# Attention and routed feed-forward block: the first head group's rows made by tripled weights, batch 1 projected in step 0

## The chip, the cores and the metric

The kernel runs on one core of a Trainium2 chip. The metric is the device time of one execution in microseconds (us), given as the median of several executions. A core has five engines that work side by side, each through its own list of instructions in order: TensorE (PE in the profile; PEld is its loading of weights), VectorE (DVE), ScalarE (ACT), GpSimd (POOL) and SyncE (SP, which here only issues DMAs). They wait for each other through semaphores.

## The reference

A transformer block on x (4 batches, 256 tokens, 128 channels) with 64 context tokens per batch. All is float32.

```
q, k, v = heads(LN(x) @ W + b)                 # 16 heads of 8 channels
y  = softmax(causal(q k^T / sqrt(8))) v        # self attention
y += softmax(qc kc^T / sqrt(8)) vc             # keys and values from the context
x  = x + y @ Wp + bp
h  = LN(x); top 8 of 32 experts by sigmoid(h @ Wr + br)
x  = x + shared(h) + sum_e w_e * expert_e(h)   # silu(h Wg) * (h Wu) @ Wd
```

## The kernel before

Attention goes in 16 steps: step i is batch `b = i // 4` and head group `g = i % 4`, four heads at a time. For each step there are four products on TensorE: `natural(i)` gives scores with queries on the partitions, from which VectorE takes the row maxima (`maxima(i)`: three reductions, of self tile 0, self tile 1 and the context); `turn_max(i)` turns them, ScalarE's `shift(i)` writes them as four more rows of the queries; `scores(i, c)`, c = 0 to 3, gives the shifted scores with keys on the partitions, ScalarE takes the exponential (`exps`), POOL masks it; `attend_self` and `attend_context` multiply with the values. In the loop, step i of TensorE holds scores(i), turn_max(i+1), natural(i+2) and attend(i-1), and behind natural the work in `tail_at[i]`.

A number is kept as two halves of fewer bits, hi and lo. A product of two such is three products, hi*hi, hi*lo, lo*hi (`product3`). Queries and keys of a head group have only 32 channels, so the three products are stacked into one: `query_rows` and `key_rows` hold 96 rows, each channel three times with the halves that belong together, and 4 rows for the maxima. The rows are placed by DMA from `queries` and `keys`, three DMAs per group and kind, from the queues of SP, POOL and ScalarE. `expand(i)` then makes `key_blocks` for step i: a copy of the key rows for each of the four heads, with the other heads' rows multiplied by 0 of `head_mask`. VectorE (later POOL) does heads 0 and 1, ScalarE 2 and 3. `expand_ctx(g)` does the same for the context keys, once per group for all batches. The ring has four slots, so `expand(4)` is the block of step 4, the first of batch 1.

The queries, keys and values of batches 0 and 1 are projected ahead of the loop. ScalarE rounds to the hi half with the bias added (`round_qkc`), VectorE makes the lo half (`split_qkc`), and `place_batch` has SP place the rows. Batch 2 and 3 follow as tails: `x_pair` turns the four normed tiles of both, then `keys_queries` and `cross_values` project. `run_idle(n, bank)` is n matmuls of zeros, whose results nobody reads.

After the loop comes the routed feed-forward part, to which nothing is changed.

## Time and profile before

| what | us |
|---|---|
| median of 3 executions | 203.08 (202.93 to 204.57) |
| the profiled execution | 202.79 |
| its span (first to last instruction) | 201.0 |
| TensorE busy | 187.7 (93%) |
| VectorE busy | 151.2 (75%) |
| ScalarE busy | 137.0 (68%) |
| POOL busy | 111.5 (55%) |

The span is what the trace covers; the execution adds 1.79 us around it. All starts are counted from the span's beginning. Of the span the attention steps take the part up to about 105, the feed-forward part the rest.

### The profile page before, as it was taken

What the parts mean: (1) busy time and instruction counts of PE and PEld (TensorE: products, weight loads), DVE (VectorE), ACT (ScalarE), POOL (GpSimd) and SP (SyncE); (2) the same over time, 40 slices, a digit from 0 to 9 for tenths busy, and PEclk for the clock granted to TensorE, in tenths of its full rate; (3) what the DMA queues carried; (4) which work ended last, traced back from release to release, by engine and by line L of the source; (5) the groups of instructions that cost most, each with busy time, mean ns of one, the idle gap of its engine ahead of it and who ended that gap; (6) DMA issues with size and microseconds to landing.
All of it is one profiled execution on the core that took longest, in us unless ns stands there. A gap on an engine that the chain in (4) does not pass through costs nothing.

```text
span 201.0 us, 4004 instructions
## 1 busy us (share of the span) xinstructions
PE 187.7 (93%) x1254; PEld 138.2 (69%) x1254; DVE 151.2 (75%) x345; ACT 137.0 (68%) x276; POOL 111.5 (55%) x181
## 2 busy tenths in 40 slices
PE   7969999999999999989998999599799999999993
PEld 2537677777777677767674777388588888887662
DVE  2999997566578756995574699659867888887982
ACT  3546898787898879997779455665555656555571
POOL 7899994475595799659455476674512233000020
PEclk9999999999999999999999999999999999999998
DMA  4464323232352233301302112110000000000003
GB/s 112 107 154 122 104 73 85 55 76 77 75 127 66 71 81 93 92 0 42 78 5 49 29 39 55 44 41 2 2 0 3 0 0 0 0 2 3 0 0 104
DMA packets 20434, 10.40 MB, mean 52 GB/s; under 512 B 11881, under 2 KB 18542, under 8 KB 20414
## 3 DMA queue, kind: packets, MB, share of 16 engines
q1 hardware_dynamic: 19290, 9.24, 18.1%
q0 software_dynamic: 672, 0.69, 1.4%
q10 hardware_dynamic: 452, 0.23, 0.5%
q8 instruction: 10, 0.16, 0.4%
q14 instruction: 10, 0.08, 0.1%
HBM read 4.51 MB, written 0.52 MB: 25 GB/s over the span
## 4 chain that ended last, share of the span: by engine, by line
PE 67%; POOL 13%; issue 7%; DVE 6%; ACT 4%; DMA 1%; DVEq 0%; POOLq 0%; ACTq 0%
PE psum L1394 10%; PE psum L1395 9%; PE psum L1396 9%; PE psum L1495 5%; PE psum L1551 5%; PE psum L1588 4%; PE psum L1576 4%; POOL hid_lo L732 4%; PE psum L1598 3%; PE psum L1494 3%; PE psum L1556 3%; POOL ckey_rows L450 3%; PE psum L1724 2%; PE psum L1560 2%; POOL key_rows L436 2%
## 5 line engine op out<-in xcount | busy, mean ns | idle before, releaser
L968 ACT ACTIVATE gate<-psum,bias_cols 128x512 f32<-128x512 f32 (+2 forms) x35 | 23.6, 676 | 29.1 <-PE psum L1396 29.0
L836 ACT ACTIVATE probs<-psum 128x512 f32<-128x512 f32 x64 | 36.3, 596 | 2.3 <-PE psum L1556 1.2
L732 POOL TENSOR_TENSOR hid_lo<-hid,hid_hi 128x512 fp32r<-128x512 f32 x13 | 16.8, 1289 | 31.0 <-ACT hid_hi L977 30.9
L1338 DVE SCALAR_TENSOR_TENSOR gated<-psum,bias_cols,gate 128x512 f32<-128x512 f32 x32 | 24.0, 749 | 11.3 <-ACT gate L968 10.4
L1350 DVE TENSOR_TENSOR hid<-gated,psum 128x512 f32<-128x512 f32 x32 | 21.9, 683 | 3.1 <-PE psum L1724 1.1
L1495 PE MATMUL psum<-key_blocks,query_rows 96*128 96x512 f32 x48 | 24.1, 545 | 0.0
L651 POOL TENSOR_TENSOR w_late_lo<-w_ffn,w_late_hi 128x384 fp32r<-128x384 f32 x11 | 12.8, 1161 | 18.9 <-ACT w_late_hi L848 18.9
L977 ACT CAST hid_hi<-hid 128x512 fp32r<-128x512 f32 (+1 forms) x33 | 20.2, 613 | 3.5 <-PE psum L1396 1.8
L1131 DVE TENSOR_REDUCE row_max<-psum 128x4 fp32r<-128x512 f32 x16 | 11.0, 689 | 13.9 <-PE psum L1495 13.9
L1135 DVE TENSOR_REDUCE row_max<-psum 128x4 fp32r<-128x1024 f32 x16 | 19.4, 1215 | 0.0
L1394 PE MATMUL psum<-xT_hi,w_late_hi 128*128 128x512 f32 x42 | 16.8, 401 | 0.0
L1395 PE MATMUL psum<-xT_lo,w_late_hi 128*128 128x512 f32 x42 | 16.4, 391 | 0.0
L1396 PE MATMUL psum<-xT_hi,w_late_lo 128*128 128x512 f32 x42 | 16.4, 391 | 0.0
L687 POOL TENSOR_SCALAR_AFFINE_SELECT probs<-probs 128x512 f32<-128x512 f32 x16 | 10.2, 637 | 10.6 <-ACT probs L836 10.4
L843 ACT COPY o_sb<-psum 128x512 f32<-128x512 f32 x16 | 9.4, 586 | 9.3 <-PE psum L1588 9.2
L773 ACT ACTIVATE key_blocks<-key_rows,head_mask 100x256 fp32r<-100x256 f32 x32 | 14.4, 499 | 1.8 <-DMA key_rows<-keys 1.8
L1017 DVE TENSOR_TENSOR hid_lo<-hid,hid_hi 128x512 fp32r<-128x512 f32 (+2 forms) x22 | 14.4, 660 | 1.0 <-ACT hid_hi L977 0.9
L691 POOL TENSOR_SCALAR_AFFINE_SELECT probs<-probs 128x512 f32<-128x512 f32 x16 | 10.2, 636 | 8.4 <-ACT probs L836 8.2
L1494 PE MATMUL psum<-causal,ident_bf 128*128 128x512 bf16 x32 | 12.4, 389 | 1.8 <-DVE key_blocks L1037 1.6
L678 POOL TENSOR_TENSOR key_blocks<-key_rows,head_mask 100x256 fp32r<-100x256 f32 x22 | 13.2, 622 | 0.0
L1724 PE MATMUL psum<-routeT,spread 128*128 128x512 f32 x32 | 12.9, 404 | 0.0
L1551 PEld LDWEIGHTS psum<-query_rows,key_blocks 100*128 100x128 f32 x64 | 8.6, 188 | 5.2 <-issue 4.4
(205 smaller groups left out, 516.6 us busy)
## 6 DMA issues: line engine op xcount, KB each, us to landing
query_rows<-queries SPq DMA_DIRECT2D x46, 64.0 KB, 2.1
key_rows<-keys SPq DMA_DIRECT2D x39, 32.0 KB, 1.9
w_ffn<-in_L_ffn_Wg SPq DMA_DIRECT2D x16, 64.0 KB, 2.0
w_ffn<-in_L_ffn_Wu SPq DMA_DIRECT2D x16, 64.0 KB, 2.2
w_ffn<-in_L_ffn_Wd SPq DMA_DIRECT2D x16, 64.0 KB, 2.1
ckey_rows<-ckeys POOLq DMA_DIRECT2D x12, 32.0 KB, 2.1
key_rows<-keys POOLq DMA_DIRECT2D x9, 32.0 KB, 2.0
x_sb<-in_x SPq DMA_DIRECT2D x2, 128.0 KB, 2.5
```

What stands on the lines that cost most here:

```text
L732: pool.tensor_tensor(hid_lo[:, n % 3, :], hid[:, n % 3, :], hid_hi[:, n % 3, :].bitcast(F32), ALU.subtract).then_inc(pool_lo_done, 1)
L836: act.activation(probs[:, i % 2, c, :], bank(B_ST + c % 2), ACT.Exp, scale=SCALE).then_inc(exp_done, 1)
L968: act.activation(gate[rows_of(n), n % 3, part], psum[of, B_GATE + n % 2, part], ACT.Silu, bias=bias_cols[of, BIAS_GATE + u:BIAS_GATE + u + ...
L977: act.copy(hid_hi[rows_of(n - 1), (n - 1) % 3, :], hid[rows_of(n - 1), (n - 1) % 3, :]).then_inc(hid_rounded, 1)
L1135: dve.tensor_reduce(to[:, 1, :], psum[:, B_NAT1:B_NAT1 + 2, :].rearrange("p k (j c) -> p j k c", j=GROUP), AX.XY, ALU.max).then_inc(max_do ...
L1338: dve.scalar_tensor_tensor(out=gated[:, n % 3, :], in0=bank(B_UP + n % 2), scalar=bias_cols[:, BIAS_UP + u:BIAS_UP + u + 1], in1=gate[:, n ...
L1350: dve.tensor_tensor(hid[:, n % 3, :], gated[:, n % 3, :], bank(B_WIDE + n % 2), ALU.mult).then_inc(hid_done, 1)
L1394: pe.matmul(dst, w_hi, x_hi, start=start, stop=False, skip_group_check=True)
L1395: pe.matmul(dst, w_hi, x_lo, start=False, stop=False, skip_group_check=True)
L1396: return pe.matmul(dst, w_lo, x_hi, start=False, stop=stop, skip_group_check=True)
L1495: return pe.matmul(to, query_rows[0:KR, b % 2, g, 0, P * q:P * (q + 1)], blocks[:, :, P * k:P * (k + 1)], start=not diagonal, stop=True, s ...
L1551: ins = pe.matmul(psum[:, to, SEQ * j:SEQ * (j + 1)], key_blocks[0:ROWS, i % RING, 2 * c + j, 0:P], query_rows[0:ROWS, b % 2, g, 0, :], st ...
```

## The change

It touches the part ahead of the steps and the first three steps.

- For group 0 of batch 0 the rows are not placed by DMA. Weights for its 32 channels are written three times side by side (`w_direct_hi`, `w_direct_lo`, 96 columns per tensor), and `project_direct(k)` makes the 96 rows of keys, queries and cross queries by three products each. ScalarE's `round_direct` writes all rows as hi halves, VectorE's `split_direct` rewrites the 32 rows that want lo halves. The rows of a group now have another arrangement for g = 0, so `head_mask` has two versions; the biases are repeated (`first_bias`).
- Batch 1 is not projected ahead of the loop but as the tail of step 0; `x_pair` moves from step 0 to step 1, and batch 2 and 3 follow one step later than before.
- The maxima of step 0 are turned in two parts, self first (`first_turn`, `first_shift`), so scores(0, 0) wait for the first part only.
- Work is dealt out anew: the context copy, the bias copy and two norms go from VectorE to ScalarE, part of the weight split and heads 0 and 1 of `expand_ctx` from VectorE to POOL, the statistics of batches 2 and 3 go behind maxima(1). Placement of group 0's context keys and group 1 and 2's keys moves to SP, of group 1's queries to POOL. The masks are made before x has landed.

```diff
-        tail_at = {0: [("x_pair", FIRST_BATCHES)]}
-        for b in range(FIRST_BATCHES, BATCH):
-            tail_at[2 * b - 3] = [("keys_queries", b)]
-            tail_at[2 * b - 2] = [("cross_values", b)]
+        tail_at = {0: [("keys_queries", 1), ("cross_values", 1)], 1: [("x_pair", 2)]}
+        for b in range(2, BATCH):
+            tail_at[2 * b - 2] = [("keys_queries", b)]
+            tail_at[2 * b - 1] = [("cross_values", b)]
...
+            sp.wait_ge(ckey_rows_set, 1)
+            sp.wait_ge(ck_rounded, 1)
+            place_ctx_keys(sp, 0, (0, 1))
+            sp.wait_ge(ck_split, 1)
+            place_ctx_keys(sp, 0, (2,))
             sp.wait_ge(qkc_rounded, 1)
-            place_keys(sp, 0, 0, (0, 1))
+            place_keys(sp, 0, 1, (0, 1))
             sp.wait_ge(qkc_split, 1)
-            place_keys(sp, 0, 0, (2,))
+            place_keys(sp, 0, 1, (2,))
+            place_keys(sp, 0, 2)
             sp.wait_ge(qkc_split, 3)
-            place_queries(sp, 0, 0, (1,))
-            for g in range(1, GROUPS):
-                place_queries(sp, 0, g)
+            place_queries(sp, 0, 2)
+            place_ctx_keys(sp, 3)
+            place_keys(sp, 0, 3)
+            place_queries(sp, 0, 3)
             place_batch(sp, 1)
...
+            place_ctx_keys(pool, 1)
+            pool.wait_ge(qkc_rounded, 3)
+            place_queries(pool, 0, 1, (0, 2))
+            place_ctx_keys(pool, 2, (0,))
+            pool.wait_ge(qkc_split, 3)
+            place_queries(pool, 0, 1, (1,))
...
+            def round_direct(k):
+
+                to = (key_rows[0:SHIFT_ROW, 0, 0, :], query_rows[0:SHIFT_ROW, 0, 0, 0, :],
+                      query_rows[0:SHIFT_ROW, 0, 0, 1, :])[k]
+                bias = ORDER[k][1] + BIAS_DIRECT
+                act.wait_ge(m_direct, k + 1)
...
+            act.wait_ge(have_neg_mean, 1)
+            norm(2)
+            norm(3)
+            expand_ctx(0)
+            round_x(1)
+            first_shift(0)
+            expand(1)
+            exps(0, (0,))
+            first_shift(1)
+            exps(0, (1,))
             expand_ctx(1)
-            exps(0, (0, 1))
+            exps(0, (2, 3))
             expand(2)
...
+                if i == 1:
+                    act.wait_ge(have_neg_mean, 2)
+                    for t in range(4, TILES):
+                        norm(t)
...
+            def project_direct(k):
+
+                tensor = ORDER[k][0]
+                product3(psum[0:SHIFT_ROW, B_DIRECT[k], 0:SEQ], w_direct_hi[:, tensor, :], w_direct_lo[:, tensor, :],
+                         xT_hi[:, tokens(0)], xT_lo[:, tokens(0)]).then_inc(m_direct, 1)
...
             natural(0)
-            project(1)
-            turn_max(0)
-            run_idle(3, B_MISC)
+            run_idle(2, B_ST)
...
+            def first_turn(s):
+
+                pe.wait_ge(max_done, 2 + s)
+                if s:
+                    pe.wait_ge(shift_placed, 1)
+                for n in (2 * s, 2 * s + 1):
+                    ins = pe.matmul(psum[0:GROUP, B_MAX, P * n:P * (n + 1)], row_max[:, 0, n, :],
+                                    ident_r[:, :], start=True, stop=True)
+                ins.then_inc(t_max, 1)
```

On ScalarE, around the first exponentials (`probs`; `x` is a normed tile of x). Before:

```order
L780 ACTIVATE ckey_blocks<-ckey_rows,head_mask 100x4x64 [waits placed_ck1]
L780 ACTIVATE ckey_blocks<-ckey_rows,head_mask 100x4x64
L836 ACTIVATE probs<-psum 128x512 [waits m_st] x2
L773 ACTIVATE key_blocks<-key_rows,head_mask 100x256 [waits pool_placed_k2]
L773 ACTIVATE key_blocks<-key_rows,head_mask 100x256
L876 ACTIVATE x<-x_sb,neg_mean,rstd 128x128 [waits have_neg_mean]
L876 ACTIVATE x<-x_sb,neg_mean,rstd 128x128
L836 ACTIVATE probs<-psum 128x512 [waits m_st] x2
```

And now, from the two blocks of `expand(1)` on:

```order
L826 ACTIVATE key_blocks<-key_rows,head_mask 100x256 [waits placed_k0_1]
L826 ACTIVATE key_blocks<-key_rows,head_mask 100x256
L910 ACTIVATE probs<-psum 128x512 [waits m_st]
L902 CAST query_rows<-psum 4x256 [waits t_max]
L910 ACTIVATE probs<-psum 128x512 [waits m_st]
L835 ACTIVATE ckey_blocks<-ckey_rows,head_mask 100x4x64 [waits placed_ck1]
L835 ACTIVATE ckey_blocks<-ckey_rows,head_mask 100x4x64
L910 ACTIVATE probs<-psum 128x512 [waits m_st] x2
```

The context blocks of group 1 (`placed_ck1`), first of all before, now stand behind two exponentials and a shift, and these wait for TensorE (`m_st`, `t_max`).

On VectorE, behind the maxima of group 2, the first three rows of each. Before:

```order
L1131 TENSOR_REDUCE row_max<-psum 128x4 [waits m_nat,t_max]
L1140 TENSOR_REDUCE row_max<-psum 128x8 [waits m_nat]
L1135 TENSOR_REDUCE row_max<-psum 128x4 [waits m_nat]
L1017 TENSOR_TENSOR xT_lo<-psum,xT_hi 128x512 [waits xT_rounded]
L1037 TENSOR_SCALAR key_blocks<-key_rows,head_mask 100x256 [waits m_st,placed_k1_0]
L1037 TENSOR_SCALAR key_blocks<-key_rows,head_mask 100x256
```

And now:

```order
L1232 TENSOR_REDUCE row_max<-psum 128x4 [waits m_nat,t_max]
L1241 TENSOR_REDUCE row_max<-psum 128x8 [waits m_nat]
L1236 TENSOR_REDUCE row_max<-psum 128x4 [waits m_nat]
L1114 SCALAR_TENSOR_TENSOR neg_mean<-moments,rstd 128x4 [waits have_rstd]
L1176 SCALAR_TENSOR_TENSOR keys<-psum,bias_cols,keys 128x256 [waits qkc_rounded]
L1176 SCALAR_TENSOR_TENSOR queries<-psum,bias_cols,queries 128x256 [waits qkc_rounded] x2
L1171 TENSOR_TENSOR value<-psum,b_wide 128x32x8 [waits m_v]
L1144 TENSOR_SCALAR key_blocks<-key_rows,head_mask 100x256 [waits m_st,placed_k1_0]
L1144 TENSOR_SCALAR key_blocks<-key_rows,head_mask 100x256
L1232 TENSOR_REDUCE row_max<-psum 128x4 [waits m_nat,t_max]
```

The lo halves of batch 1's keys and queries are made here, and the next rows wait for the placement of batch 1's first keys (`placed_k1_0`).

On TensorE, the end of step 1, from `scores(1, 2)` on. Before:

```order
L1556 MATMUL psum<-query_rows,key_blocks 128x128 [waits exp_done]
L1556 MATMUL psum<-query_rows,key_blocks 128x128 x3
L1560 MATMUL psum<-query_rows,ckey_blocks 128x256 [waits exp_done]
L1560 MATMUL psum<-query_rows,ckey_blocks 128x256
L1394 MATMUL psum<-xT_hi,w_qkv_hi 128x256 [waits xT_split]
L1395 MATMUL psum<-xT_lo,w_qkv_hi 128x256
```

And now:

```order
L1677 MATMUL psum<-query_rows,key_blocks 128x128 [waits exp_done]
L1677 MATMUL psum<-query_rows,key_blocks 128x128 x3
L1681 MATMUL psum<-query_rows,ckey_blocks 128x256 [waits exp_done]
L1681 MATMUL psum<-query_rows,ckey_blocks 128x256
L1736 MATMUL psum<-ident,x 128x128 [waits x_normed,qkc_split]
L1736 MATMUL psum<-ident,x 128x128 x3
L1699 MATMUL psum<-probs,value 9x256 [waits have_value,qkc_split,selected,have_cvalue]
L1699 MATMUL psum<-probs,value 9x256 x3
```

The projection of batch 2's keys gave way to the turn of the four tiles, which waits for all eight normed tiles (`x_normed`), and attend(0) is queued behind it.

## Rows read from the trace of the kernel before

**Rows 1.** The page, part 2: TensorE in 40 slices, busy tenths of each
```profile
PE   7969999999999999989998999599799999999993
```

**Rows 2.** Chain in order of time: start us, us, what
```profile
31.52 0.56 PE psum L1588 x4
...
37.26 0.56 PE psum L1588 x4
...
42.74 0.56 PE psum L1588 x4
...
48.49 0.56 PE psum L1588 x4
...
53.26 0.56 PE psum L1588 x4
```

**Rows 3.** Windows: stretch, then busy us (instructions) by engine, granted clock, DMA
```profile
20.00:22.00 2.00, 2.00 (x12) 1.21 (x12) 2.00 (x6) 2.00 (x6) 2.00 (x5) 1.00 0.47 122
```

**Rows 4.** Timeline of TensorE and VectorE, 8 to 33: start, us, what, [idle before]
```profile
8.01 0.70 PE L1456 MATMUL psum<-ctxT,w_ctx 64*128 64x256 f32 x2
...
14.56 0.38 PE L1494 MATMUL psum<-causal,ident_bf 128*128 128x512 bf16 x1 [1.56 <-DVE key_blocks L1037]
...
19.30 0.74 PE L1551 MATMUL psum<-query_rows,key_blocks 100*128 100x256 f32 x4
...
26.28 1.22 DVE L1135 TENSOR_REDUCE row_max<-psum 128x4 fp32r<-128x1024 f32 x1
...
32.02 0.73 PE L1551 MATMUL psum<-query_rows,key_blocks 100*128 100x256 f32 x4
```

**Rows 5.** Timeline of ScalarE, 17 to 23
```profile
18.59 0.57 ACT L828 CAST query_rows<-psum 4x512 fp32r<-4x512 f32 x1 [0.17 <-PE psum L1537]
...
20.00 1.07 ACT L836 ACTIVATE probs<-psum 128x512 f32<-128x512 f32 x2
20.96 0.90 ACT L773 ACTIVATE key_blocks<-key_rows,head_mask 100x256 fp32r<-100x256 f32 x2
21.75 0.87 ACT L876 ACTIVATE x<-x_sb,neg_mean,rstd 128x128 f32<-128x128 f32 x2
```

**Rows 6.** SP timeline, and the tile key_rows up to 35 us
```profile
18.54 1.78 SPq L436 DMA_DIRECT2D key_rows<-keys  x3
...
DMA to landing us min/median/max: 1.7/1.9/3.4
```

**Rows 7.** Timeline of POOL, 22 to 27
```profile
22.52 4.71 POOL L619 TENSOR_TENSOR ckey_blocks<-ckey_rows,head_mask 100x256 fp32r<-100x256 f32 x8
```

**Rows 8.** VectorE groups by form, 8 to 35: xcount, busy us, mean ns
```profile
L1135 DVE TENSOR_REDUCE row_max<-psum 128x4 fp32r<-128x1024 f32 x4 | 4.9, 1216 | 0.0
L1037 DVE TENSOR_SCALAR key_blocks<-key_rows,head_mask 100x256 fp32r<-100x256 f32 x10 | 4.2, 457 | 0.0
L1131 DVE TENSOR_REDUCE row_max<-psum 128x4 fp32r<-128x512 f32 x5 | 3.4, 686 | 1.5 <-PE psum L1495 1.5
...
L1072 DVE SCALAR_TENSOR_TENSOR queries<-psum,bias_cols,queries 128x256 fp32r<-128x256 f32 x5 | 2.3, 477 | 0.1
```

**Rows 9.** TensorE fillers (timeline), and windows after its last matmul
```profile
1.26 2.31 PE L1434 MATMUL psum<-fill 128*128 128x512 bf16 x5 [1.26 <-DVE fill L1050]
...
3.98 1.42 PE L1434 MATMUL psum<-fill 128*128 128x512 bf16 x4
...
9.73 1.69 PE L1434 MATMUL psum<-fill 128*128 128x512 bf16 x7
...
199.00:200.00 1.00, 0.00 (x0) 0.00 (x0) 0.00 (x0) 0.00 (x0) 0.00 (x0) 0.66 0.75 222
200.00:201.00 1.00, 0.00 (x0) 0.00 (x0) 0.00 (x0) 0.00 (x0) 0.00 (x0) 0.50 0.13 41
```

**Rows 10.** Timeline: SP and POOL at the bias bp
```profile
36.92 1.25 SPq L546 DMA_DIRECT2D b_wide<-in_L_xattn_bp  x1
...
42.63 0.88 POOL L631 TENSOR_TENSOR x_sb<-x_sb,b_wide 128x128 f32<-128x128 f32 x2
```

More of the change, by code:

```diff
@@ L443, in place_queries, with place_ctx_keys @@
                 half = QUERY_PARTS[part]
-                eng.dma_start(query_rows[rows_of_part(part), b % 2, g, :, :].bitcast(F32),
-                              queries[mine, half, b, :, :].bitcast(F32)).then_inc(placed_q[b % 2][g], 16)
-        def place_ctx_keys(eng, g):
-            for part, half in enumerate(KEY_PARTS):
-                eng.dma_start(ckey_rows[rows_of_part(part), g, :].bitcast(F32),
+                eng.dma_start(query_rows[rows_of_part(part, g), b % 2, g, :, :].bitcast(F32),
+                              queries[mine, half, b, :, :].bitcast(F32)).then_inc(queries_of(b, g)[0], 16)
+        def place_ctx_keys(eng, g, parts=range(PARTS)):
+            for part in parts:
+                half = KEY_PARTS[part]
+                eng.dma_start(ckey_rows[rows_of_part(part, g), g, :].bitcast(F32),
                               ckeys[PART * g:PART * (g + 1), half, :].bitcast(F32)).then_inc(placed_ck[g], 16)
@@ new lines, in _ @@
+            act.wait_ge(t_bias, 1)
+            act.copy(bias_cols[:, BIAS_Q:BIAS_ROWS], bank(B_BIAS, 2 * BIAS_DIRECT)).then_inc(have_bias_cols, 1)
+            act.wait_ge(have_bias_cols, 1)
+            act.wait_ge(m_ck, 1)
+            act.activation(ckeys[:, 0, :], bank(B_CK, CTX_KEYS), ACT.Identity,
+                           bias=bias_cols[:, BIAS_CK:BIAS_CK + 1]).then_inc(ck_rounded, 1)
+            round_direct(0)
+            round_direct(1)
+            round_qkc(0, 0)
+            expand(0)
@@ L1004, in chain, with measure @@
                 dve.wait_ge(v_chain, chained[0])
-            def norm_stats(src, tiles, done):
+            def measure(src, tiles):
                 for k in range(tiles.start, tiles.stop):
@@ L1009, in norm_stats, with spread_of @@
                 chain(ins)
+            def spread_of(tiles, done):
                 for k in range(tiles.start, tiles.stop):
@@ L1252, in long_part @@
                                       ALU.subtract).then_inc(route_ready, 1)
+            maxima(0)
+            split_x(1)
             dve.wait_ge(t_ffn_bias, 1)
             dve.tensor_copy(bias_cols[:, 0:2 * UNITS],
[L1256 to L1268 removed]
+                            psum[:, B_MISC, SEQ:SEQ + 2 * UNITS]).then_inc(have_ffn_bias, 1)
+            values(0)
+            maxima(1)
             expand(2)
[L1270 removed]
+            stats_of(2)
             cvalues()
@@ L1605, in tail @@
                           "route_turn": routeT_ready}[name]
-                take_misc(reader, 3 * b + 2 if name == "keys_queries" else b + 1)
+                if (name, b) == ("cross_values", 1):
+                    pe.wait_ge(have_value, 1)
+                else:
+                    take_misc(reader, 3 * b + 2 if name == "keys_queries" else b + 1)
                 if name == "x_pair":
```

388 lines of the change are left out of this document (214 added, 174 removed).

## The prediction

> **What bounds the kernel now.** First the page's slices of 5 us [rows 1]: TensorE stands at 9 in nearly all of them. Then the chain of waits in order of time [rows 2]: from 27.5 on it runs through TensorE alone, step after step at TensorE's own pace. From one attend's context product (L1588) to the next it takes 4.77 us where no tail lies between, 5.48 us with `keys_queries`, 5.74 with `cross_values` [rows 2]. So the first tail is worth 0.71 us, the second 0.97, and the steps have no slack in which to hide either. Ahead of 27.5 it is otherwise: the windows show VectorE busy without a break [rows 3], while TensorE is kept busy with fillers. Whatever VectorE or a placement loses or gains there goes to the end undiminished. The marks of the kernel before are in the timeline [rows 4]: first masked product 14.56; first scores 19.30; end of VectorE's maxima of group 2 at 27.50, which I call **T**, since the third turn waits for it; scores of step 2 at 32.02. From that last mark on the work is the same before and after, but for the one tail named below. The question is thus when the changed kernel comes to that mark.
>
> **The front.** Up to the turned x nothing is moved that is read late. In TensorE's queue the context key product (0.70 us, [rows 4]) now lies ahead of the first projection, which I put at 7.45. Two direct products end at 8.2, two normal ones at 8.9, 0.36 us each. ScalarE rounds each 0.4 us later; VectorE's lo halves of the direct keys and queries end at 8.8 and 9.2 (0.48 a piece, [rows 8]), its two blocks at 9.85, ScalarE's two at 10.05 (0.90 a pair, [rows 5]). No row DMA is in this path any more: three issues and 1.9 us to landing are saved. First masked product: 10.1 against 14.56. POOL's new subtractions of 256 and 96 columns, at the 0.6 us that it takes for 256 [rows 7], end by 8.6, ahead of their reader; uncovered they would cost under 0.5.
>
> Next VectorE has the maximum of tile 0 from 10.75, two splits, the maximum of tile 1 (1.22, [rows 8]), to 13.5, and TensorE turns at 13.95. POOL has seven DMA issues and then two multiplications of 0.6 [rows 7], so the context products of group 0 come at 14.35; two fillers; first scores at **15.3** against 19.30. The lead is 4.0 us.
>
> **Where the lead goes.** In ScalarE's new order the context blocks of group 1 stand behind two exponentials and a shift. Scores at 15.3 give the first exponential at 15.65; group 1's first masked product is at 15.95 and the second half of the maxima is turned by 16.65; shift to 17.05 (half of a 0.57 one, [rows 5]), exponential to 17.6, two blocks to 18.5 (0.90). TensorE's context products of group 1 are ready at 16.6 and wait until 18.55. VectorE's reductions stand behind that. From 19.1 it has two of them to 21.0, `expand(2)` 0.65, `stats_of(2)` 1.4 (it stood earlier before), `cvalues` 0.86, `expand(3)` 1.0, three reductions 2.6: T' = **27.6**, and no lead is left. From below it is bound by VectorE's own work from 10.7 on: nine reductions 7.8, three splits 1.4, three pairs of blocks 2.5 [rows 8], and 3.3 for the rest (0.42, 0.18, 0.41, 0.86, 1.4), in all 15.0, so T' is not under 25.7. From above by a late landing of POOL's `query_rows` (up to 3.4 us at the tile `key_rows`, of which POOL placed a part, [rows 6]): 28.5. I take 27.6, which follows the order.
>
> **The new wait.** Before, batch 1's keys were placed from 18.54 on [rows 6], and `expand(4)` of step 1 never waited. Now VectorE splits them behind the maxima of group 2, to T'+0.6. SP issues three `key_rows`, the third 1.2 us after the first (three in 1.78), which lands 1.9 later [rows 6]: T'+3.8. ScalarE's `expand(4)` waits for that and takes 0.90; behind it stand four norms of `x`, 1.7 (two took 0.87, [rows 5]): T'+6.4. TensorE has done its other work of step 1 by T'+2.5 (as before, from 27.50 to 30.0) and stands at `x_pair`, which wants all eight normed tiles. This is a stall of **3.9 us** with no cover, since attend(0) is queued behind it. `x_pair` takes 0.5 and attend(0) 1.3, so step 2's scores come at T'+8.3. Before they came at T+4.52, and a `keys_queries` of 0.71 was done by then which now lies ahead. **Difference: (T'-T) + 8.3 - 4.52 + 0.71 = (T'-T) + 4.5.** With T' = 27.6 that is +4.6; with its bounds +2.7 and +5.5. A landing at 1.7 or 2.2 moves it by 0.3.
>
> **The clock.** TensorE's last matmul ends at 198.0. The granted clock is 0.66 of full in 199 to 200 and 0.50, the 1.2 GHz level, in the next [rows 9]; so it fell less than 2 us after the work stopped, and the new stall is twice that. The price: the first five fillers took 2.31 us, four from 3.98 took 1.42, seven from 9.73 took 1.69 [rows 9], 0.46, 0.36 and 0.24 each. A matmul costs twice as much at the low level, and that level was left some 3.5 us after the first. Bounds: 0 if it does not fall, 1.75 (3.5 us of work at half speed). I take 1.0, as part of the low time falls into the stall itself.
> The Trainium skill, TensorE: Matmul & The Clock Gate, section "HAM oscillation — how this bites in real kernels", says that waits for data of this length put the engine back to the low clock each time. By that rule, with the start's 3.5 us in full, the sum would be 0.75 higher, 209.4; without it 207.7.
>
> **Later on.** SP comes 9.6 us late to batch 1 (28.2 for 18.54), and since it paused there before, some 9 us late to the bias `bp`: issued at 45.8 for 36.92 [rows 10], landing 3.7 later at 49.5. POOL's `add_bp` of step 3, at 42.63 before [rows 10] and 47.2 now, waits 2.3 us for it. Behind it are POOL's block for step 7 and masks of step 4, whose reader attend(4) ends at 53.26 before [rows 2] and is thus wanted at 57: covered. Uncovered it would cost 1 to 2 us. I cost it at nothing.
>
> **Sum.** The profiled execution took 202.79 us with a span of 201.0. After: 202.79 + 4.6 + 1.0 = 208.4 (span 206.6). The median shown, 203.08, is 0.3 above that execution, so the forecast for the median is **208.6**.
>
> **Rivals.**
> (a) The clock holds through the stall. For it: the clock held over TensorE's wait of 1.56 us ahead of 14.56 [rows 4]. Against: this one is over twice as long. 203.08 + 4.6 = 207.7.
> (b) VectorE's work alone sets T', because ScalarE comes to the context blocks sooner than laid out here: T' = 25.7, +2.7, with a fall of the clock up to +3.7, 205.8 to 206.8.
> (c) The other side: batch 1's keys lie ready when `expand(4)` asks, and TensorE's own work sets the pace from its first scores. From 19.30 to 32.02 it took 12.7; batch 1's projection adds 1.7 (0.71 + 0.97), the turn in two parts 0.2, `keys_queries` takes 0.71 away: 13.9. From 15.3 that is 29.2, with 0.71 still ahead 29.9, so -2.1, 201.0. It decides for faster only if T' is under 27.5 - 4.5 = 23.0, and VectorE's own list ends at 25.7. It needs my durations to be a fifth too long.
> (d) The stall is half as long, since ScalarE's norms or the split run ahead of where the order has them: near +1, 204.
> (e) More than forecast: POOL's queries late, `add_bp` uncovered, the low clock for longer, 211.
>
> **How the numbers follow.** Forecast 0.42, (a) 0.22, (b) 0.13, (c) 0.05, (d) 0.08, (e) 0.10. A measurement of this kernel tells 1% (2 us) from no change. Faster is (c), 0.05; within 1% is (d) and a little of (b), 0.11; slower is the rest, 0.84. The range from 205.2, a little under (b), to 210.8 leaves out (c), (d) and most of (e).
>
> **What would show it.** In the profile after: first masked product near 10.1, first scores near 15.3; TensorE idle about 2 us ahead of group 1's context products, released by ScalarE's `ckey_blocks`; the turn for group 2 at 27.6; ScalarE waiting for the DMA of `key_rows` at `expand(4)`; TensorE idle near 4 us ahead of `x_pair`, released by ScalarE's `x`; a granted clock under 1.0 in the few us behind it; the scores of step 2 at 35.9 or, by the clock, up to 1 later. I am wrong if those stand before 32, or if `expand(4)` does not wait.

## The result: 4.8% slower, against a forecast of 2.7%

The changed kernel takes 213.25 us (median of 4, 212.52 to 214.61) against 203.65 us for the kernel before in the same rounds (median of 4, 202.93 to 204.57): ratio 1.0477, interval 1.0403 to 1.055. The forecast was 208.6 us with a range up to 210.8. The direction and both waits were foreseen, the size was not: 9.6 us instead of 5.5.

The page of the changed kernel (span 211.4 us, 213.14 with what lies around it), part 2, TensorE's busy tenths and granted clock in slices of 5.3 us:

```profile
PE   7895993999999999998999899699989999999993
...
PEclk9999588599999999999999999969999999999997
```

TensorE is nearly as busy as in [rows 1], but its clock fell three times: in the fifth and sixth slice, in the seventh and eighth, and once in the feed-forward part (slice 27). The first two falls follow two waits. The timeline shows both, with the marks that answer to [rows 4]:

```profile
10.66 0.38 PE L1596 MATMUL psum<-causal,ident_bf 128*128 128x512 bf16 x1 [0.34 <-DVE key_blocks L1144]
...
14.45 2.22 DVE L1144 TENSOR_SCALAR key_blocks<-key_rows,head_mask 100x256 fp32r<-100x256 f32 x2
...
15.44 0.83 PE L1672 MATMUL psum<-query_rows,key_blocks 100*128 100x256 f32 x4
...
16.77 0.38 PE L1596 MATMUL psum<-causal,ident_bf 128*128 128x512 bf16 x1 [0.51 <-DVE key_blocks L1144]
...
18.64 0.89 ACT L835 ACTIVATE ckey_blocks<-ckey_rows,head_mask 100x256 fp32r<-100x256 f32 x2
...
19.68 0.47 PE L1630 MATMUL psum<-ckey_blocks,query_rows 96*128 96x256 f32 x2 [1.95 <-ACT ckey_blocks L835]
20.19 0.69 DVE L1241 TENSOR_REDUCE row_max<-psum 128x8 fp32r<-128x512 f32 x1 [1.44 <-PE psum L1630]
...
27.59 1.22 DVE L1236 TENSOR_REDUCE row_max<-psum 128x4 fp32r<-128x1024 f32 x1
...
29.53 0.48 DVE L1176 SCALAR_TENSOR_TENSOR keys<-psum,bias_cols,keys 128x256 fp32r<-128x256 f32 x1 [0.65 <-ACT queries L856]
...
30.09 1.78 SPq L469 DMA_DIRECT2D key_rows<-keys  x3
...
33.62 0.91 ACT L826 ACTIVATE key_blocks<-key_rows,head_mask 100x256 fp32r<-100x256 f32 x2 [1.60 <-DMA key_rows<-keys]
34.44 1.63 ACT L950 ACTIVATE x<-x_sb,neg_mean,rstd 128x128 f32<-128x128 f32 x4
36.21 1.09 PE L1736 MATMUL psum<-ident,x 128*128 128x128 f32 x4 [3.34 <-ACT x L950]
...
39.65 1.22 PE L1672 MATMUL psum<-query_rows,key_blocks 100*128 100x256 f32 x4
```

The reader sees the forecast's whole chain. First scores come at 15.44 (forecast 15.3). ScalarE's blocks of group 1 start at 18.64 (forecast 17.6), and TensorE waits 1.95 us for them. The maxima of group 2, T', end at 28.81. Batch 1's keys are issued at 30.09, `expand(4)` waits for them, the four norms stand behind it, and TensorE waits 3.34 us at `x_pair`. But step 2's scores come at 39.65, not 35.9, and the four take 1.22 us instead of 0.73 in [rows 4]. The windows tell why. (Each line has the stretch, its length, then the busy time of TensorE, its weight loads, VectorE, ScalarE and GpSimd, each with its number of instructions; then the granted clock and two numbers on DMA.)

```profile
20.00:22.00 2.00, 2.00 (x13) 1.63 (x12) 1.80 (x2) 0.72 (x2) 1.73 (x4) 0.85 0.37 88
...
26.00:28.00 2.00, 2.00 (x9) 1.50 (x8) 1.95 (x4) 0.48 (x2) 1.94 (x5) 0.50 0.00 0
...
34.00:36.00 2.00, 0.00 (x0) 0.00 (x0) 2.00 (x4) 2.00 (x7) 0.00 (x0) 0.76 0.28 71
...
40.00:42.00 2.00, 2.00 (x11) 1.68 (x11) 0.00 (x0) 1.59 (x4) 0.00 (x0) 0.53 0.33 82
42.00:44.00 2.00, 2.00 (x17) 1.78 (x16) 1.76 (x5) 1.35 (x4) 0.63 (x1) 1.00 0.28 71
```

The clock fell behind either wait and stood at 0.50, the 1.2 GHz level, from 21.4 to 28.2 and from 35.0 to 41.9: 6.8 us each, most of it with TensorE at work. The third low stretch, from 137.5 to 140.9, was half as long.

Of three kernels below (ctx_first, loads_first, loads_quiet) the profiled execution was a disturbed one, so their marks behind the first 40 us say less than their medians, and the median of the undisturbed executions is 208.34 us for ctx_first, 205.28 for loads_first and 205.08 for loads_quiet.

### The profile page after: what moved, and what is told of

It is laid out like the page before. It is cut to its first block, busy times and chain, and to the rows that moved or that the text cites. A ratio compares the mean times of both kernels' runs of the same rounds, so it can differ in the third digit from the quotient of the medians.

```text
span 211.4 us, 4023 instructions
## 1 busy us (share of the span) xinstructions
PE 193.5 (92%) x1256; PEld 143.1 (68%) x1256; DVE 154.2 (73%) x341; ACT 140.1 (66%) x286; POOL 109.0 (52%) x175
## 3 DMA queue, kind: packets, MB, share of 16 engines
q1 hardware_dynamic: 19674, 9.37, 17.9%
## 4 chain that ended last, share of the span: by engine, by line
PE 69%; issue 8%; DVE 6%; ACT 5%; POOL 5%; DMA 3%; SPq 1%; POOLq 1%; DVEq 0%; ACTq 0%
PE psum L1492 10%; PE psum L1493 9%; PE psum L1494 9%; PE psum L1597 5%; PE psum L1672 5%; PE psum L1711 4%; PE psum L1699 4%; POOL hid_lo L784 4%; PE psum L1596 4%; PE psum L1721 3%; PE psum L1677 3%; PE psum L1846 2%; PE psum L1681 2%; PE psum L1656 2%; PE psum L1630 2%
## 5 line engine op out<-in xcount | busy, mean ns | idle before, releaser
L1597 PE MATMUL psum<-key_blocks,query_rows 96*128 96x512 f32 x48 | 25.3, 570 | 0.0
L739 POOL TENSOR_SCALAR_AFFINE_SELECT probs<-probs 128x512 f32<-128x512 f32 x16 | 10.1, 634 | 12.9 <-ACT probs L910 12.7
L1596 PE MATMUL psum<-causal,ident_bf 128*128 128x512 bf16 x32 | 13.2, 413 | 1.1 <-DVE key_blocks L1144 0.9
L1672 PEld LDWEIGHTS psum<-query_rows,key_blocks 100*128 100x128 f32 x64 | 9.1, 197 | 5.2 <-issue 4.8
```

The lines of the kernel that those rows point to most:

```text
L1596: pe.matmul(to, ident_bf[:, :], causal[:, :, :], start=True, stop=False, skip_group_check=True)
L1597: return pe.matmul(to, query_rows[0:KR, b % 2, g, 0, P * q:P * (q + 1)], blocks[:, :, P * k:P * (k + 1)], start=not diagonal, stop=True, s ...
L1672: ins = pe.matmul(psum[:, to, SEQ * j:SEQ * (j + 1)], key_blocks[0:ROWS, i % RING, 2 * c + j, 0:P], query_rows[0:ROWS, b % 2, g, 0, :], st ...
```

## The experiments

All runs but two (before_ffn and before_ffn2, which start from the kernel before) start from the changed kernel. First scores of a step, from the timelines (us), and the medians, each beside the kernel before in its own rounds.

| kernel | step 0 | step 1 | step 2 | step 6 | step 15 | median | before |
|---|---|---|---|---|---|---|---|
| before | 19.30 | 26.39 | 32.02 | 53.76 | 101.63 | | |
| after | 15.44 | 29.42 | 39.65 | 63.06 | 110.90 | 213.25 | 203.65 |
| fill1 | 15.94 | 27.52 | 38.83 | 62.40 | 110.21 | 209.91 | 204.25 |
| fill2 | 15.79 | 29.82 | 38.35 | 60.75 | 108.59 | 209.98 | 204.25 |
| fill12 | 15.66 | 27.22 | 36.93 | 59.35 | 107.19 | 209.50 | 204.25 |
| norms_first | 15.44 | 29.43 | 35.61 | 58.54 | 106.36 | 209.19 | 204.25 |
| ctx_first | 15.44 | 25.38 | 36.71 | 60.05 | 107.90 | 208.69 | 204.44 |
| both_orders | 15.44 | 25.40 | 32.34 | 56.50 | 104.35 | 206.81 | 204.44 |
| dve_late | 15.55 | 25.48 | 32.44 | 56.88 | 104.70 | 206.49 | 204.60 |
| loads_first | 15.65 | 25.59 | 32.56 | 55.11 | 102.99 | 205.33 | 204.54 |

### The clock: idle products in the two waits

```diff
                 if i == 1:
                     first_turn(1)
+                    run_idle(8, B_NATC)        # fill1, fill12
...
                 if name == "x_pair":
+                    run_idle(14, B_MISC)       # fill2, fill12
                     pe.wait_ge(x_normed, TILES)
```

fill1: 

> The changed kernel with 8 idle products in the first stall: after step 1's shift turn and ahead of group 1's context products (1.95 us wait at 19.68). Theory (the clock term, read together with what ends last): the stretch at 0.50 from 21.7 to 28.1 goes, but the maxima of step 2 are set by VectorE's row of work and move by under 1 us; the projection of batch 1 ends 0.5 to 1 us earlier, so the kernel gains 0.6 to 1.2 us, about 212.3. Rival A (each microsecond at the low clock costs half of itself): 6.4 us at 0.50 give 3.2 us back, about 210.0. Rival B (the clock is not lost by this stall but by the sparse work ahead of it, the awake share of 16 to 20 us): the stretch at 0.50 stays though the stall is filled, 213.2.

fill2: 

> The changed kernel with 14 idle products put into TensorE's stall in step 1, ahead of the wait for the last four normed tiles of x (the 3.34 us wait at 36.21). Nothing else moves, so that wait ends at the same time. Theory (the excess over the forecast is TensorE's clock, which fell in this stall and in the one before group 1's context products and stayed at 0.50 for 6 to 7 us each time): the clock does not fall at 36 us, the rest of step 1 (36.2 to 41.9, of which some 5.7 us at 0.50) runs at full clock and the kernel gains 2.9 us, so about 210.4 us; the first scores of step 2 come near 37.8 instead of 39.65. Rival (the waits alone make the loss, since what runs at the low clock lies beside other engines' work): within 0.5 us of the changed kernel.

fill12: 

> Both sets of idle products, in the stall before group 1's context products and in the stall before the last four tiles of x. Theory (clock): the clock shows one low stretch less for each, the kernel stands 3.5 to 4.1 us below the changed one, about 209.5, which is the forecast's 208.6 plus the 1.2 us by which the maxima of step 2 came late. Rival A (every low microsecond costs half): 6.4 us below, 206.9. Rival (waits alone): within 0.5 us.

Measured: fill1 209.91 us, fill2 209.98, fill12 209.50. Windows of fill2, whose scores of step 2 came at 38.35:

```profile
34.00:36.00 2.00, 2.00 (x11) 0.87 (x9) 2.00 (x5) 2.00 (x6) 0.00 (x0) 1.00 0.33 82
36.00:38.00 2.00, 1.88 (x24) 0.92 (x24) 1.04 (x2) 1.81 (x4) 1.07 (x2) 1.00 0.27 70
```

The clock holds through the wait for x, and fill2 gains 3.3 us where 2.9 was expected: the rival "waits alone" is out. fill12 has no dip ahead of the feed-forward part and lies where the theory put it; so the two falls cost 213.25 - 209.50 = 3.75 us (4.35 if each is taken against the kernel before in its own rounds). The profiled executions of fill2 and fill12 have no dip in the feed-forward part either and differ by 209.58 - 208.18 = 1.4 us: that is the first fall, and some 2.4 are left for the second. fill1 is half a miss. Its profiled execution (212.50 us) behaves as the theory says: T' did not move, and the clock still fell at `x_pair`. Its three other executions took 209.6 to 210.1, at mean clocks of 0.980, 0.987 and 0.992, which is a larger gain than the first fall's share. A stretch of 6.8 us at 0.50 lowers the mean over 208 us by 0.016, so the two at 0.987 and 0.992 cannot hold one: there the second low stretch was shorter or absent. Why, no record shows. Rival B (sparse work ahead of the wait is the cause) is out, since the low stretch went with the wait filled.

### Two places in ScalarE's queue

```diff
-            exps(0, (0,)); first_shift(1); exps(0, (1,)); expand_ctx(1)      # ctx_first
+            expand_ctx(1); exps(0, (0,)); first_shift(1); exps(0, (1,))
...
-                expand(i + 3);  [i == 1: norm(4) .. norm(7)]                 # norms_first
+                [i == 1: norm(4) .. norm(7)];  expand(i + 3)
```

norms_first: 

> The changed kernel with ScalarE's norms of tiles 4 to 7 ahead of its expansion of step 4's key blocks, so that they no longer stand behind the DMA of batch 1's keys (landed near 33.6). Theory (the stall at x_pair is this queue: projection, split, DMA, expansion, norms): ScalarE reaches the norms at about 31.6, x is there at 33.2, TensorE goes on near 33.7 instead of 36.2, the scores of step 2 come at 35.5 to 36 and the clock does not fall there; 5 us less than the changed kernel, about 208.2; the expansion itself ends near 35.5 and is first needed in step 4. Rival (the wait is only handed on: the expansion ends late and step 4's scores, or VectorE behind its own expansion, wait instead): 2 us or less, 211 or more.

ctx_first: 

> The changed kernel with ScalarE's two context key blocks of group 1 ahead of the first exponential, instead of behind two exponentials and the shift of step 1. Theory (this place in ScalarE's queue is where the lead is lost): they run at 15.9 to 16.8, the context products follow the second turn of the shift at once (17.7 instead of 19.68), TensorE's 1.95 us wait there and the clock's fall behind it go, VectorE's wait of 1.44 us at 20.19 goes, so the maxima of step 2 end at about 27.3 instead of 28.8; the x_pair stall stays and comes 1.5 to 2 us earlier, with its fall. 2 to 2.5 us less than the changed kernel, about 210.9. Rival (the maxima of step 2 are set by VectorE's work beside it, not by that wait): the stall goes but the scores of step 2 move by less than 0.8 us; 212.5 to 213. A miss would also be the first exponential 0.9 us later costing as much as is won.

both_orders: 

> Both orders of ScalarE: context blocks of group 1 ahead of the first exponential, and norms 4 to 7 ahead of the expansion of step 4's key blocks. Theory (two queue places on ScalarE make the loss and both low stretches): no fall of the clock before 44 us, maxima of step 2 at about 27.3, scores of step 2 at 33 to 33.6 (32.02 in the kernel before), 2 to 2.5 us below norms_first's 209.2, so 206.5 to 207.2. Rival (once norms come first, something else is last for x_pair, so that the earlier maxima give nothing): 209, as norms_first.

Measured: norms_first 209.19 us, 1 us short of its theory; ctx_first 208.69, 2.2 us better than its theory; both_orders 206.81, as its theory has it. (ctx_first lost the first low stretch and with it 4.0 us at the scores of step 1.) Lines of both_orders:

```profile
15.81 0.89 ACT L835 ACTIVATE ckey_blocks<-ckey_rows,head_mask 100x256 fp32r<-100x256 f32 x2
...
25.87 1.22 DVE L1236 TENSOR_REDUCE row_max<-psum 128x4 fp32r<-128x1024 f32 x1
...
28.67 1.64 ACT L950 ACTIVATE x<-x_sb,neg_mean,rstd 128x128 f32<-128x128 f32 x4
...
30.45 0.63 PE L1736 MATMUL psum<-ident,x 128*128 128x128 f32 x4 [0.83 <-ACT x L950]
30.80 0.61 DVE L1144 TENSOR_SCALAR key_blocks<-key_rows,head_mask 100x256 fp32r<-100x256 f32 x2 [2.14 <-DMA key_rows<-keys]
```

Nothing was computed faster or left out. The blocks of group 1 moved from 18.64 to 15.81, T' from 28.81 to 27.09, the wait at `x_pair` shrank from 3.34 to 0.83 us, and step 2's scores stand at 32.34, 0.3 behind the kernel before. Order alone took back 6.4 of the 9.6 us, the two low stretches with it. The last line shows a third place: now VectorE waits 2.14 us at its own half of `expand(4)`, with the maxima of step 3 behind it.

### VectorE and GpSimd at the same time

The changed kernel's pair of key blocks at 14.45 took 2.22 us, against 0.62 at 9.68. GpSimd multiplied and issued DMAs at that time (multiplications to 14.76, two DMA issues to 15.74, multiplications again from 15.75).

```diff
             expand_ctx(0, range(2))
-            place_ctx_keys(pool, 2, (1, 2))
+            pool.wait_ge(v_blocks_set, 4)      # pool_quiet, all_orders only
             expand_ctx(1, range(2))
+            place_ctx_keys(pool, 2, (1, 2))    # pool_later, three_orders too
```

pool_later: 

> The changed kernel with GpSimd's last two DMA issues of group 2's context key rows behind its multiplications for group 1 instead of ahead of them, so that none is issued at 14.71 to 15.74, where VectorE's two key block multiplications for step 1 took 2.22 us (0.62 us at 9.68). Theory (the DMA issues of GpSimd slow VectorE there): the pair takes 1.3 us or less and the natural scores of step 1 start 0.9 to 1.5 us earlier, near 15.5 instead of 16.77; the stall ahead of the context products stays and moves with them, 1 us less in all, about 212.2. Rival (it is GpSimd's multiplications on the same memory port): the multiplications now lie where the issues lay, and the pair still takes 2 us or more; the time stays at 213.2.

three_orders: 

> All three orders: context blocks first and norms first on ScalarE, DMA issues of group 2's context rows later on GpSimd. Theory: the gains add, since each lies on the way to the maxima of step 2 or to x_pair: scores of step 2 at 32 to 32.6, no low clock, 205.5 to 206.2 (1 us below both_orders). If it stands at or above both_orders, either the slow pair was not the issues' doing or VectorE was not last for the natural scores of step 1.

Measured: 217.07 and 210.12 us, 3.8 and 3.3 slower than without the edit. My theory fell. The pair took 3.82 us in both, TensorE waited 2.11 us for it, and the clock fell in that wait and stood at 0.50 for some 10 us (17.9 to 28.0 in pool_later, 18.1 to 28.3 in three_orders), so the loss is the collision and the clock together. The timeline of pool_later, GpSimd and VectorE:

```profile
13.57 2.32 POOL L660 TENSOR_TENSOR ckey_blocks<-ckey_rows,head_mask 100x256 fp32r<-100x256 f32 x4
...
14.44 3.82 DVE L1144 TENSOR_SCALAR key_blocks<-key_rows,head_mask 100x256 fp32r<-100x256 f32 x2
...
15.85 1.03 POOL L484 DMA_DIRECT2D ckey_rows<-ckeys  x2
...
16.86 1.25 POOL L668 MEMSET cvalue<- 128x1312 f32 x1
```

The pair's first half ended at 16.99 (14.44 + 2.55) and its second at 18.26, each just after one of GpSimd's pieces (16.88 and 18.11). VectorE did not come in between GpSimd's multiplications, which followed each other without a gap, nor ahead of the DMA issues behind them. A third theory, that it is GpSimd's work of any kind in SBUF, was then tried:

pool_quiet: 

> The changed kernel in which GpSimd, after its two multiplications for group 0, waits until VectorE's two key block multiplications for step 1 are done, then does its two for group 1, and then the two DMA issues. In the run with the issues behind the multiplications, VectorE's pair began at 14.44 and took 3.82 us, ending with GpSimd's unbroken row of multiplications, issues and memset (13.57 to 18.11). Theory (VectorE's multiplication does not get through while GpSimd works in SBUF, whatever GpSimd does): with GpSimd waiting, the pair ends 0.7 us after GpSimd's multiplication of group 0 ends at 14.76, near 15.45 instead of 16.67, the natural scores of step 1 start at 15.55 instead of 16.77, everything behind comes 1.2 us earlier, 212.0 us or a little less. Rival (the multiplication itself is slow there, for its data or its place): the pair keeps 2.2 us and GpSimd's work comes late, 213.5 or more.

dve_late: 

> Both orders of ScalarE, and in step 1 VectorE's maxima of step 3 ahead of its half of step 4's key block expansion, which waits 2.14 us for batch 1's keys in that kernel (30.80) with the maxima of step 3 behind it; scores of step 3 there come 6.36 us after those of step 2, against 5.74 in the kernel before. Theory (one more place in a queue where something ready stands behind the late keys): the maxima of step 3 end by 31.5 instead of 33.75, scores of step 3 come 5.5 to 5.7 us after those of step 2, 0.7 to 0.9 us less than both_orders' 206.8, so 206.0. Rival (TensorE is full there, and the wait costs nothing): 206.8.

all_orders: 

> All four queue places mended: ScalarE's two, VectorE's expansion of step 4 behind its maxima of step 3, and GpSimd's wait until VectorE's pair for step 1 is done. Theory: the gains add: scores of step 2 at 31.1 to 31.4 (32.02 in the kernel before), no low clock ahead of the feed-forward part, 204.6 to 205.2. It does not beat the kernel before, since the loop then holds the projection of batch 1, which stood ahead of the loop there, and its lead of 4 us in the first scores has shrunk to under 1 us by step 2. Rival (the rest of the loss is in the loop): 206 or more.

Measured: pool_quiet 211.36 (209.52 to 213.95), dve_late 206.49, all_orders 207.26. In pool_quiet the pair took 0.74 us and group 1's context products came at 18.95 instead of 19.68. But T' came only at 28.65 for 28.81, since the next pair took 1.62 us instead of 0.96. Most of what its profiled execution gained at step 1's scores (11.40 us behind the first ones instead of 13.98) is the clock, which there held through the same wait of 1.95 us. The timeline of all_orders, whose theory (204.6 to 205.2) failed:

```profile
14.47 0.74 DVE L1145 TENSOR_SCALAR key_blocks<-key_rows,head_mask 100x256 fp32r<-100x256 f32 x2
...
19.15 2.37 POOL L660 TENSOR_TENSOR ckey_blocks<-ckey_rows,head_mask 100x256 fp32r<-100x256 f32 x4
19.45 2.21 DVE L1145 TENSOR_SCALAR key_blocks<-key_rows,head_mask 100x256 fp32r<-100x256 f32 x2
```

With GpSimd waiting, the pair takes 0.74 us: that part is shown. But the next pair ran into GpSimd's four multiplications for group 2 and took 2.21 (0.96 in both_orders), and nothing was left of the gain: scores of step 1 at 25.70 against 25.40. The Trainium skill, SBUF — State Buffer, section "Who interferes with whom", says that when a VectorE instruction runs in a mode that uses two ports (a tensor_scalar can), it contends with GpSimd: the one that issues first gets the shared pair of ports for its whole instruction, and the other is blocked. The runs agree that the one that came second was held, and go further: in pool_later VectorE's instruction, begun at 14.44, was held over the rest of GpSimd's four multiplications and the two DMA issues behind them. That it is this port, and not something else that the two share, no run here separates. dve_late (VectorE's maxima of step 3 ahead of its half of `expand(4)`) mended the gap from step 2 to step 3, 5.73 us for 6.36, but a longer one opened from step 5 to 6, 7.5 us, so it gained only 0.3, which the spread of the executions (205.16 to 207.23) does not tell from nothing.

### The loads on SyncE's queue, and the clock in the feed-forward part

GpSimd's and SyncE's lines of dve_late, which answer to [rows 10]:

```profile
44.26 0.59 SPq L585 DMA_DIRECT2D w_qkv<-in_L_xattn_Wp  x1
...
46.63 0.35 SPq L591 DMA_DIRECT2D b_wide<-in_L_xattn_bp  x1
...
49.87 0.87 POOL L679 TENSOR_TENSOR x_sb<-x_sb,b_wide 128x128 f32<-128x128 f32 x2 [6.79 <-DMA b_wide<-in_L_xattn_bp]
```

```diff
+            sp.dma_start(w_qkv[:, 4, :], w["Wp"]) ... Wr, bd, bp, br     # loads_first and all below
             place_batch(sp, 1)
-            sp.dma_start(w_qkv[:, 4, :], w["Wp"]) ... Wr, bd, bp, br
...
+            pool.wait_ge(v_blocks_set, 6)   # loads_quiet: ahead of the DMA issues; expand(2) ahead of maxima(1)
...
+                            run_idle(6, 6)  # loads_ffn, before_ffn: ahead of the first down projection
```

loads_first: 

> The kernel with both orders of ScalarE and VectorE's late expansion (206.5 us), and on SyncE's queue the seven loads of Wp, Wr, bd, bp and br ahead of the placing of batch 1, where the queue is idle from 21.4 to 27.7 us, instead of behind it at 44.26. In that kernel GpSimd waited 6.79 us for bp (until 49.87), key blocks stood behind it, and the scores of step 6 came 7.5 us after those of step 5 (5.74 in the changed kernel, 4.8 in the kernel before). Theory (the backlog on SyncE's queue, which the forecast took at nothing, costs as soon as the rest of the lead is there): the wait goes, scores of step 6 come 5.0 to 5.8 us after those of step 5, 1.7 to 2.4 us less: 204.2 to 204.9. Rival (the batch's own placing is as late and holds the same key blocks): the gap shrinks by under 0.5 us; 206.2.

loads_quiet: 

> As the kernel with the loads first, and GpSimd kept out of VectorE's way at both places: it waits for VectorE's key blocks of step 1 before its multiplications for group 1, and for those of step 2, which now stand ahead of VectorE's maxima of step 1, before its DMA issues and memsets. In the run where only the first place was mended the pair for step 1 took 0.74 us instead of 2.22, but the pair for step 2 took 2.21 beside GpSimd's four multiplications of group 2, and nothing was left. Theory: both pairs take 0.8 us or less, natural scores of step 2 start near 21.0, scores of step 1 at 24.6 instead of 25.5; 0.6 to 1 us less than with the loads first alone. Rival (GpSimd's own four multiplications for group 2, now until 22.5, become last for the context products of step 2): no gain, or 0.5 us more.

loads_ffn: 

> As the kernel with the loads first, and six idle products ahead of the first down projection of the feed-forward part, into the 1.69 us wait for GpSimd's lower halves of hid (131.06 in the kernel without loads first; 127.97 in the kernel before). In the runs so far the mean clock was 0.98 to 1.00 in the kernel before and the time went with it (1.000: 203.3, 0.988: 204.6, 0.981: 206.0). Theory (this one wait makes the clock fall in some runs and not in others, in either kernel, about 1.2 us each time): all runs show a clock of 0.995 or more, and the median is about 1 us less than with the loads first, with a spread under 0.5 us. Rival (the fall is not this wait's): no change of the median or of the clock.

before_ffn: 

> The kernel before with the same six idle products ahead of its first down projection. Theory: its median falls from 204.5 on this chip to 203.3 or less, with mean clocks of 0.995 or more in all runs; that part of the difference between kernels is then the clock's chance at this wait, and not the change. Rival: no change.

Measured: loads_first 205.33 us (theory 204.2 to 204.9), ratio 1.002 (0.9987 to 1.0053), no difference from the kernel before. GpSimd's long wait is gone and step 6 follows step 5 after 5.74 us. loads_quiet 205.38, ratio 1.0053: its rival was right. The two pairs took 0.75 and 0.61 us, as the theory has it, but GpSimd's four multiplications, made to wait, came at 22.23 to 24.60, VectorE's third pair ran into them (2.32 us), and TensorE waited for them:

```profile
24.65 0.79 PE L1633 MATMUL psum<-ckey_blocks,query_rows 96*128 96x256 f32 x2 [3.23 <-POOL ckey_blocks L659]
```

loads_ffn 206.02 and before_ffn 205.39: 0.7 and 0.9 us slower than without the products, both groups of clocks still there. That edit was misplaced: the first down projection waits for nothing. The wait is at the fifth item:

```diff
                         if m == 4:
+                            pe.wait_ge(*misc_read[-1])
+                            run_idle(6, B_MISC)
                         pe.wait_ge(*lo_done(m))
```

norms_split starts from loads_first, and split_ffn2 is norms_split with these idle products:

```diff
+                if i == 0: negative_mean(2)          # VectorE: ahead of maxima(2), not behind it
...
+                    if i == 1: norm(4); norm(5)      # ScalarE: ahead of shift(2)
                     shift(i + 1)
                     exps(i, (1,))
+                if i == 1: norm(6); norm(7)          # ahead of expand(4)
```

norms_split: 

> The kernel with the loads first (205.3 us, like the kernel before), and x's last four norms earlier: VectorE forms their means ahead of its maxima of step 2 (24.8 instead of 27.2), and ScalarE does two of the norms ahead of the shift of step 2, where it stood idle for about 1 us, and two behind the second exponential. Theory (at x_pair TensorE still waits 0.8 us for the last norm): that wait goes, the shift comes 0.5 us later, scores of step 2 come 0.4 to 0.8 us earlier, 204.7 to 205.0. Rival (the shift is what natural scores wait for, or the loop is full of TensorE's own work): no change or 0.3 us more.

before_ffn2: 

> The kernel before, with the six idle products now in the wait itself: ahead of the fifth item's down projection, which waits 1.69 us at 127.97 for GpSimd's lower halves of hid (the run before had them ahead of the first down projection, which waits for nothing, and so only added 1.1 us). Theory (this wait makes the clock fall in some runs): mean clocks of 0.995 or more in all runs, no run in the group at 0.986 to 0.989, median near 203.2 instead of 204.5. Rival (the clock falls elsewhere, or for a cause outside TensorE's own waits): both groups of runs remain.

split_ffn2: 

> Norms split, and the six idle products in the wait of the fifth item's down projection. Theory: 203.5 to 203.9 in all runs, 0.9 to 1.3 us below norms_split's median and below the median of the kernel before. Rival: as norms_split.

Measured: before_ffn2 **203.03 us** (202.90 to 203.32) beside 204.41 for the kernel before, ratio 0.9938 (0.9916 to 0.9961), mean clocks 0.996 to 1.000. split_ffn2 204.21 (0.9997, interval 0.9974 to 1.0021; 1.2 us below norms_split as expected, 0.3 above its range), norms_split 205.43 (1.0053, a miss). The wait in the kernel before, and in the changed kernel with the clock behind it:

```profile
127.97 0.50 PE L1394 MATMUL psum<-hid_hi,w_ffn_hi 128*128 128x512 f32 x1 [1.69 <-POOL hid_lo L732]
```

```profile
137.25 0.64 PE L1492 MATMUL psum<-hid_hi,w_ffn_hi 128*128 128x512 f32 x1 [1.69 <-POOL hid_lo L784]
...
138.00:140.00 2.00, 1.54 (x7) 0.84 (x6) 0.51 (x1) 0.37 (x1) 1.39 (x2) 0.50 0.23 53
```

The fillers of before_ffn2 and a stretch behind them:

```profile
126.58 1.47 PE L1434 MATMUL psum<-fill 128*128 128x512 bf16 x6
...
130.00:132.00 2.00, 1.93 (x10) 1.62 (x11) 0.42 (x1) 1.47 (x5) 1.15 (x2) 1.00 0.40 98
```

The clock held behind this wait in the profiled execution of the kernel before (202.79 us, granted clock 1.00 from 128 to 132) and fell in the profiled one of the changed kernel. By the execution times it falls in most executions: the 23 of the kernel before in these rounds fall into five of 202.90 to 203.12 us (clock 0.995) and eighteen of 204.00 to 205.66 (0.981 to 0.992). With the wait filled, none of before_ffn2's six executions is in the second group. norms_split removed the wait at `x_pair`, but TensorE then waited 1.10 us (0.62 before that edit) for VectorE's maxima of step 2, which now stand behind the means, and 0.50 us more for an exponential: the wait moved, and nothing was won.

## Why the prediction was right in its chain and wrong in its size

- **Front.** First masked product 10.66 for 10.1: the projection began at 7.41 as laid out (7.45), but VectorE's second lo half ended at 9.65 for 9.2 and its blocks at 10.30 for 9.85. First scores 15.44 for 15.3. Right.
- **Where the lead goes.** Right in place and releaser: TensorE waits 1.95 us for ScalarE's `ckey_blocks` (forecast 1.95), and ctx_first shows that this queue place is the cause: step 1's scores 4.0 us earlier. The mark is off: T' 28.8 for 27.6. The products came at 19.68 for 18.55. The natural scores of step 1, at 16.77 for 15.95, stood behind a pair of blocks that took 2.22 us, where my 2.5 for three pairs gives 0.8 each, and from there the list ran as laid out. I had GpSimd's rows beside VectorE's and priced each alone. T' is 1.2 us late by this, but the slow pair is not shown to be all of it: pool_quiet, without it, has the products 0.7 us earlier and T' 0.2.
- **The new wait.** Right: `expand(4)` waits for `key_rows`, the norms stand behind it, TensorE stands 3.34 us at `x_pair` (3.9). norms_first confirms the order as the cause. Of the formula, (T'-T) + 4.5, the second part held: with the clock kept, in fill12, step 2's scores stand at 36.93 = T' + 8.0, for T' + 8.3.
- **The clock: the term that failed.** The prediction took 1.0, with bounds 0 and 1.75, from 3.5 us of work at half speed, behind one stall. It fell behind two, for 6.8 us each time, and fill12 measures 3.75 us; with that in place of 1.0 the forecast would have been 211.4, out of its range, while the late T' alone gives 209.8. Two errors are in this. The smaller, some 1.4 us: the wait of 1.95 us, which the prediction itself had found, was never given a price. It is paid through batch 1's projection, which ran at the low clock until 28.2: VectorE waited 0.65 us for its results and split the keys from 29.53 on, where fill12 has them at 28.91 without a wait. The larger, 2.4 us for 1.0: the length of the low stretch was read from the start of the kernel, [rows 9], as 3.5 us, and part of it was put into the stall itself. But the clock fell only at 35.0, 1.2 us ahead of the stall's end at 36.2, so most of the low stretch lay on work. And it was twice as long. That length is not fixed: the runs show low stretches of 3.4 us too, so 3.5 was one of the lengths that occur, and its being chosen was the bet. The rule of the Trainium skill (TensorE: Matmul & The Clock Gate, section "HAM oscillation — how this bites in real kernels") pointed the right way, up, and the second fall, behind a wait of 3.34 us, agrees with it; with my 3.5 us it gave 209.4, also too little.
- **Later on.** Costed at nothing, and rightly so in the changed kernel, where the step from 5 to 6 takes 5.74 us. But the cover was the loss itself: once the two stalls were mended, GpSimd waited 6.79 us for `bp`, and moving the loads gave 1.2 us.
- **The sum with measured terms:** 203.65 + 1.3 (T'-T) + 4.5 + 3.75 = 213.2, against 213.25. The 3.75 is itself taken from 213.25, so what this tests is the rest: 203.65 + 1.3 + 4.5 = 209.45, against fill12's 209.50.
- **Rivals.** (a), the clock holds, and (b), T' at 25.7, did not happen. (d) was priced wrongly: half the stall gone is 2 us less of the 4.6, so 205.7 by the prediction's own sum and not 204. (e), 211, came nearest and had the cause, "the low clock for longer", at a chance of 0.10; of its other two parts neither happened. (c), faster, did not happen, but its view that the front gives a real lead has something in it: with the places mended, the lead in step 0's scores is 3.65 us, in step 1's 0.8, and at step 2 it is 0.5 behind. How that divides between the projection of batch 1, now inside the loop, and VectorE's row of work was not measured; the 0.8 us wait at `x_pair` is not shown to be it, since norms_split removed it and TensorE then waited elsewhere.

No version with the change beat the kernel before. The best one without idle products, loads_first, equals it, and so does split_ffn2 with them (ratio 0.9997). The kernel before with the same six idle products is 1.2 us faster than split_ffn2 and 0.6% faster than without them.

## What to carry to other kernels

When a change makes one thing late, go through every queue that waits for it and look for what is ready but stands behind that wait: here ScalarE, VectorE and GpSimd (by SyncE's loads) each had such a place, and order alone was worth 8 of 9.6 us. Price a TensorE wait of the size at which the traces show a fall (here from 1.7 us on, not each time) twice, once for itself and once for the clock, and fill those that cannot be removed. Idle products must stand in the wait itself, or they only add time, 0.7 to 0.9 us here. A wait that is covered in the slow version can be bare in the mended one, so read the trace anew after each repair.

## What the runs showed of the hardware

- The clock fell behind waits of 1.95, 3.34 and (in most executions) 1.7 us, and held over 1.56 us in [rows 4]; in pool_quiet's profile it held over the same wait of 1.95 us ahead of group 1's context products, and in the profile of the kernel before over 1.69 us at 127.97. A fall need not come within the wait: in the changed kernel the first came at 21.4, 1.7 us after TensorE was at work again.
- Where it fell it stayed at the 1.2 GHz level for 3.4 us (before_ffn from 130.0, both_orders from 132.3, pool_quiet from 35.7, the changed kernel from 137.5), for 6.8 us (both stalls of the changed kernel, fill1 from 34.4) or for some 10 us (pool_later from 17.9), with TensorE at work for most of it. The rows do not tell what decides in the single execution.
- Two groups of execution times 1.4 us apart (medians 203.01 and 204.43), in one and the same kernel, came from one wait of TensorE; six idle products of 1.47 us in all removed the upper group, and the median 203.03 is that of the lower one.
- A pair of VectorE's multiplications in SBUF took 0.62 us alone, 0.74 to 1.05 beside part of GpSimd's, and 1.6 to 3.8 when it began within a row of them. Keeping GpSimd away only moved the collision to the next pair or, in loads_quiet, to the one after.
